# Graph-attention scores as 32-row products on four row groups, without head stacks

## What is computed

```python
q = (x @ Wq.T).reshape(b, n, NUM_HEADS, HEAD)        # 12 heads of 32
k = (x @ Wk.T).reshape(b, n, NUM_HEADS, HEAD)
bias = (spatial_encoding + edge_encoding)[:, None]   # adj + adj
scores = jnp.einsum('bqhd,bkhd->bhqk', q, k) * scale + bias
scores = jnp.where(row_nonzero, scores, -jnp.inf)
p = jax.nn.softmax(scores, axis=-1)
out = jnp.einsum('bhqk,bkhd->bqhd', p, v).reshape(b, n, h)
return out @ Wo.T + bo
```

## Time and profile before

| | us |
|---|---|
| median of 3 runs | 1613.49 (1613.08 to 1613.63) |
| the profiled execution, device time | 1610.95 |
| its span in the trace | 1608.7 |
| TensorE busy, of the span | 1530.1 (95%) |
| VectorE busy | 1247.8 (78%) |
| ScalarE busy | 900.9 (56%) |
| GpSimd busy | 470.3 (29%) |
| one group in the steady state, for example 801.05 to 848.64 | 47.59 |

### The profile page before, as it was taken

How to read it: one execution, slowest core, us unless ns; L and a number is a source line. 1 busy time by engine, 2 the same in 40 slices (tenths; PEclk the granted TensorE clock), 3 DMA queues, 4 the chain that set the end, 5 groups by cost and what they waited for, 6 DMA issues and landing times.

```text
span 1608.7 us, 38829 instructions
## 1 busy us (share of the span) xinstructions
PE 1530.1 (95%) x13760; PEld 1501.6 (93%) x13760; DVE 1247.8 (78%) x4559; ACT 900.9 (56%) x2091; POOL 470.3 (29%) x926
## 2 busy tenths in 40 slices
PE   4799999999999999999999999999999999999984
PEld 4799999999999999999999999999999999999973
DVE  6568887778887777888777888777788877788753
ACT  4556566556556555656655665655565665566531
POOL 4113332233323223333223332313333322332222
PEclk8799999999999999999999999999999999999986
DMA  8222022222112222212222211222221222221100
GB/s 246 61 63 71 31 51 73 70 73 73 49 39 63 74 70 73 67 30 55 74 70 73 73 44 44 64 71 72 73 65 30 57 73 70 74 73 35 40 10 10
DMA packets 84637, 101.66 MB, mean 63 GB/s; under 512 B 6640, under 2 KB 84208, under 8 KB 84448
## 3 DMA queue, kind: packets, MB, share of 16 engines
q1 hardware_dynamic: 83872, 98.20, 22.6%
q0 software_dynamic: 576, 0.99, 0.3%
HBM read 61.41 MB, written 37.75 MB: 62 GB/s over the span
## 4 chain that ended last, share of the span: by engine, by line
PE 90%; ACT 5%; DVE 2%; issue 1%; DMA 1%; POOL 1%; SPq 0%; DVEq 0%; ACTq 0%; POOLq 0%
PE bank L355 72%; PE bank L430 5%; PE bank L361 4%; PE bank L423 3%; PE bank L414 3%; ACT c_sb L556 3%; PE bank L436 1%; ACT qk L495 1%; PE bank L448 0%; DMA pT<-w 0%; DMA k<-qk_parts 0%; ACT prob L519 0%; DMA x_sb<-x 0%; DVE c_sb L645 0%; DVE weights L582 0%
## 5 line engine op out<-in xcount | busy, mean ns | idle before, releaser
L355 PE MATMUL bank<-h,weights 128*128 128x256 f32 x3456 | 429.8, 282 | 5.4 <-DVE h L758 5.0
L355 PEld LDWEIGHTS bank<-h,weights 128*128 128x128 f32 x3456 | 412.4, 190 | 6.4 <-issue 5.7
L519 ACT ACTIVATE prob<-prob,rmin 128x128 f32<-128x128 f32 x768 | 240.3, 390 | 13.3 <-DVE rmin L675 13.3
L355 PE MATMUL bank<-weights,h 128*128 128x384 f32 x1152 | 228.7, 343 | 0.0
L355 PE MATMUL bank<-hA,weights 128*128 128x256 f32 x1728 | 218.8, 281 | 1.5 <-DVE hA L606 1.5
L606 DVE TENSOR_TENSOR n<-bank,n 128x512 fp32r<-128x512 f32 x192 | 128.5, 683 | 109.9 <-ACT n L495 109.8
L355 PEld LDWEIGHTS bank<-hA,weights 128*128 128x128 f32 x1728 | 210.9, 189 | 1.9 <-DVE hA L606 1.9
L355 PEld LDWEIGHTS bank<-weights,h 128*128 128x128 f32 x1152 | 193.9, 188 | 0.0
L817 POOL TENSOR_SCALAR less_mean_gnn<-mv_gnn 128x2 f32<-128x2 f32 x64 | 14.4, 225 | 582.0 <-DVE mv_gnn L611 582.0
L495 ACT ACTIVATE n<-bank 128x512 fp32r<-128x512 f32 x192 | 113.9, 594 | 117.6 <-PE bank L355 117.6
L675 DVE CUSTOM_DVE_ANT_0 prob<-bank,adj_sb 128x128 f32<-128x128 f32 x768 | 174.5, 286 | 0.1
(11 more groups left out here) (109 smaller groups left out, 2660.3 us busy)
## 6 DMA issues: line engine op xcount, KB each, us to landing
qk_parts<-qk SPq DMA_DIRECT2D x96, 256.0 KB, 2.4
q<-qk_parts SPq DMA_DIRECT2D x96, 192.0 KB, 4.6
k<-qk_parts SPq DMA_DIRECT2D x96, 192.0 KB, 5.5
x_sb<-x SPq DMA_DIRECT2D x32, 384.0 KB, 4.1
out<-x SPq DMA_DIRECT2D x32, 384.0 KB, 2.5
adj_sb<-adj SPq DMA_DIRECT2D x32, 128.0 KB, 2.1
prob<-w SPq DMA_DIRECT2D x4, 576.0 KB, 7.2
x<-w SPq DMA_DIRECT2D x3, 576.0 KB, 4.8
```

The lines of the kernel that those rows point to most:

```text
L355: mm = pe.matmul(out, lhsT, rhs, start=(n == 0), stop=(n == len(pairs) - 1))
L519: e = act.activation(prob[:, j, h, :], prob[:, j, h, :], ACT.Exp, bias=rmin[:, j, h:h + 1], scale=-1.0)
```

## The change

The stacks in DRAM and the SBUF tiles `q3`, `k3` are gone, with all of their DMAs and waits. `qk` gets a second buffer, and `xn1`, which lay in it, a tile of its own. The scores of a graph are made by 36 products of 32 rows straight from the q and k parts of `qk`: head h = c*4 + a lies in rows 32a to 32a+31, so four products in a row go to four row groups and four banks; three of them in a bank (over n) sum up to a head. All 36 are issued at the fourth step of a graph (`S{j}3`); the first three only wait for their banks. A bank now holds the three heads of one row group, so scores, exps and transposed probabilities come in 4 jobs of 3 heads for each graph where there were 3 jobs of 4. Lists and banks are new on all engines.

```diff
-        qk = sb("qk", [P, 2, 2 * C, T], F16)
-        xn1 = qk[...]
-        qk_dram = nc.dram_tensor("qk_parts", [2, P, 2, 2 * C, T], F16).ap()
-        q3 = sb("q3", [3 * D, NH, T], F16)
-        k3 = sb("k3", [3 * D, NH, T], F16)
+        qk = sb("qk", [P, 2, 2, 2 * C, T], F16)
+        xn1 = sb("xn1", [P, G, H])
...
     "SP": [
-        ("k3", 1), ("ld_adj", 2), ("out", -1), ("qs0", 2), ("qs1", 2), ("qs2", 2), ("ld_x", 3), ("q3", 2)],
+        ("ld_adj", 2), ("out", -1), ("ld_x", 3)],
...
                 elif step[0] == "S":
-                    j, c = int(step[1]), int(step[2])
-                    pe.wait_ge(s_q3, STACKED * (g + 1))
-                    pe.wait_ge(s_k3, STACKED * (g + 1))
-                    for a in range(HC):
-                        mm = pe.matmul(bank(step)[:, a * P:(a + 1) * P], q3[:, a * C + c, j * P:(j + 1) * P], k3[:, a * C + c, j * P:(j + 1) * P], start=True, stop=True)
-                    mm.then_inc(full(step), 1)
+                    j, last = int(step[1]), int(step[2])
+                    if last == HC - 1:
+                        for k in range(3):
+                            wait_drained(pe, f"QK{k}", g)
+                        js = slice(j * P, (j + 1) * P)
+                        for c in range(C):
+                            for n, (u, v) in enumerate(PARTS):
+                                for a in range(HC):
+                                    rs = slice(a * D, (a + 1) * D)
+                                    mm = pe.matmul(bank(f"S{j}{a}")[:, c * P:(c + 1) * P], qk[rs, g % 2, u, c, js], qk[rs, g % 2, v, C + c, js],
+                                                   start=(n == 0), stop=(n == len(PARTS) - 1))
+                                    if (c, n) == (C - 1, len(PARTS) - 1):
+                                        mm.then_inc(full(f"S{j}{a}"), 1)
...
                 elif step[0] == "P":
-                    for a in range(HC):
-                        mm = pe.transpose(bank(step)[:, a * P:(a + 1) * P], prob[:, j, c * HC + a, :], ident[:, :])
+                    for c in range(C):
+                        mm = pe.transpose(bank(step)[:, c * P:(c + 1) * P], prob[:, j, c * HC + a, :], ident[:, :])
...
-                    lo(step, g, pT[:, LO, hs, :], pT[:, HI, hs, :], HC * P, "p (h q) -> p h q", h=HC)
+                    lo(step, g, pT[:, LO, a:NH:HC, :], pT[:, HI, a:NH:HC, :], C * P, "p (h q) -> p h q", h=C)
```

More of the change, by code:

```diff
@@ L71 @@
 BANK = {
-    0: ["S02", "C10", "N01", "P10", "C01", "V0"],
-    1: ["N10", "S00", "S12", "C11", "AT", "OT0"],
-    2: ["N12", "S01", "S10", "HL00", "QK1"],
-    3: ["HL11", "P00", "P11", "PV1", "QK2"],
-    4: ["HL10", "P01", "PV0", "HL01", "C00", "HTa"],
-    5: ["T2a", "N00", "U0", "T1b", "OT1", "WO1", "V1"],
-    6: ["N11", "U1", "N02", "P12", "WO0", "HTb"],
-    7: ["T2b", "S11", "P02", "T1a", "QK0"],
+    0: ["S01", "S13", "HL00", "WO0", "V0"],
+    1: ["C10", "N00", "P02", "P10", "QK1", "N10"],
+    2: ["N02", "S12", "P01", "P13", "HTb", "WO1", "T2a"],
+    3: ["V1", "N01", "P00", "PV0", "OT1", "N11", "U1"],
+    4: ["S00", "S10", "T1b", "P12", "QK2", "T2b"],
+    5: ["HL11", "C11", "S02", "HL01", "C00", "N12"],
+    6: ["HL10", "S03", "U0", "T1a", "P11", "HTa"],
+    7: ["AT", "S11", "P03", "C01", "OT0", "PV1", "QK0"],
 }
@@ L83 @@
     "SP": [
[1 row of a table removed]
+        ("ld_adj", 2), ("out", -1), ("ld_x", 3)],
     "PE": [
[5 rows of a table removed]
-    "ACT": [
[5 rows of a table removed]
-        ("HTb", 0)],
-    "DVE": [
[9 rows of a table removed]
[6 rows of a table added]
+    "ACT": [
[6 rows of a table added]
+    "DVE": [
[9 rows of a table added]
     "POOL": [
-        ("ln1", 2), ("ml", 0), ("gn1", -1), ("mu", 0), ("za0", -1), ("za1", -1), ("zb0", -1), ("xbo1", 2), ("xbo0", 2),
-        ("zb1", -1), ("gn0", 0), ("ln2", 1)],
+        ("xbo1", 2), ("ml", 0), ("gn1", -1), ("za1", -1), ("mu", 0), ("za0", -1), ("zb1", -1), ("zb0", -1), ("xbo0", 2),
+        ("gn0", 0), ("ln2", 1), ("ln1", 3)],
 }
-SPLIT_JOBS = (["T1a", "T1b", "QK0", "QK1", "QK2", "V0", "V1"] + [f"P{j}{c}" for j in range(G) for c in range(C)] +
+SPLIT_JOBS = (["T1a", "T1b", "QK0", "QK1", "QK2", "V0", "V1"] + [f"P{j}{a}" for j in range(G) for a in range(HC)] +
               ["OT0", "OT1", "T2a", "T2b"] + [f"N{l}{k}" for l in range(L) for k in range(3)] +
@@ L247, in build @@
         SPLIT_AFTER = {
-            "ACT": {"": (0,), "xn1_1": (1,), "T1b": (2, 3), "QK0": (4, 5), "QK1": (6,), "QK2": (7,), "V1": (8,), "V0": (9,)},
-            "DVE": {"ln1_ag": (0,), "T1b": (1, 2), "QK0": (3, 4), "QK1": (5,), "QK2": (6, 7), "V1": (8,), "V0": (9,)}}
+            "ACT": {"": (0,), "xn1_0": (1,), "T1b": (2, 3), "QK1": (4, 5), "QK2": (6,), "QK0": (7,), "V0": (8,), "V1": (9,)},
+            "DVE": {"ln1_ag": (0,), "T1b": (1, 2), "QK1": (3, 4), "QK2": (5,), "QK0": (6, 7), "V0": (8,), "V1": (9,)}}
         def staged(m):
@@ L300, in load_weights @@
                     sp.dma_start(staged(m), w_d[m].rearrange("(c p) o -> p c o", p=P)).then_inc(s_wload[STAGE_OF[m]], 16)
-            def stack(dst, s, which, parts, p):
-                for r, part in enumerate(parts):
-                    heads = qk_dram[p, :, part, which * C:which * C + C, :].rearrange("(a d) c t -> d a (c t)", d=D)
-                    sp.dma_start(dst[D * r:D * r + D, :, :].rearrange("d (a c) t -> d a (c t)", a=HC), heads).then_inc(s, 16)
             def run(step, g):
@@ L418, in run @@
                     wait_drained(pe, f"V{j}", g)
-                    for c in range(C):
-                        wait_drained(pe, f"P{j}{c}", g)
+                    for a in range(HC):
+                        wait_drained(pe, f"P{j}{a}", g)
                     for h in range(NH):
@@ L679, in run @@
                     j = int(step[2])
-                    for c in range(C):
-                        wait_drained(dve, f"S{j}{c}", g)
+                    for a in range(HC):
+                        wait_drained(dve, f"S{j}{a}", g)
                     dve.tensor_scalar(row0[:, j, :], rmin[:, j, :], 0.0, None, ALU.is_equal).then_inc(s_row0[j], 1)
@@ L763, in _ @@
                     split_weights(SPLIT_AFTER["DVE"].get(step, ()))
-                    if step == "QK1":
+                    if step == "QK2":
                         make_constants()
```

64 lines of the change are left out of this document (20 added, 44 removed), and 40 rows, old and new, of the table ORDER.

## The result

The changed kernel took 1638.28 us (median of 4 runs, 1636.87 to 1638.84) against 1613.28 for the kernel before (4 runs, 1610.75 to 1613.63): a ratio of 1.0157, with an interval of 1.0139 to 1.0175. That is +25 us where +55 had been forecast. The profiled execution took 1636.87 us (span 1635.1), 25.9 more than that of before, so the trace shows the difference in full.

What follows compares the result with a forecast made beforehand. TensorE was taken as the bound, busy 47.13 of 47.59 us a group. Terms of -52, +70, +56, -14 and -5 gave +55 us on the 1613.5 median, so 1668.5 us, with a range of 1622 to 1745.

Steps and rivals of the forecast that it cites:

- old scores go, new ones come: TensorE's scores: removing the old products saves 52 us, two blocks of 32-row products a group at 1.10 us add 70.
- stall behind U0: From U0's end to OT0, VectorE's list takes 8.65 us against TensorE's 6.89: 1.8 us a group lost, +56 us.
- wait at HTb goes: TensorE's wait at HTb for ScalarE's norm, 0.47 us in a usual group, disappears: -14 us.
- fill and drain of the pipeline: Two waits for the k stack while the pipeline fills, 9.0 us together, go and are partly replaced: -5 us.
- price of a 32-row product: Score blocks on TensorE: 25 ns a product, taken from PV's pairs, so 36 products take 0.90 us a block.
- Rival (a): Score blocks: four row groups truly at once, 53 ns a set, 0.60 us a block, 1636.5 us; chance 0.16.
- Edges: Entry to and exit from each score block on TensorE, where the kind of product changes: 0.20 us a block.
- x: The x load before ln1_st, asked for a few steps earlier: landing takes 4.1 us, 0.6 us of cover, costed at nothing.
- Rival (b): Score blocks: no overlap at all between row groups, 1.9 + 0.3 us a block, 1739.5 us; chance 0.14.
- rival (d): TensorE's granted clock falls to its lower level for part of each group, +100 us or more; chance 0.04.
- group of 49.3 us: Expected sign in the trace: a steady-state group takes 49.3 us, against 47.59 before.
- rival (c): Behind U0: VectorE's path is covered, no new stall, 1612.5 us, or 1580.5 with Rival (a) besides; chance 0.16.

Runs made afterwards that it cites:

- experiment 1: Changed kernel with a graph's 36 score products ordered by row group, all nine of one before the next: 1693.0 us.
- experiment 2: Changed kernel with score products alternating over two row groups at a time, 0 and 1 for 18 products, then 2 and 3: 1654.48 us.
- experiment 3: Changed kernel with only the HI by HI score products, 12 a graph instead of 36: 1619.68 us.
- experiment 4: Changed kernel with the first graph's 36 score products split into 12 before and 24 behind the two adjacency transposes: 1644.98 us.
- experiment 5: Changed kernel with VectorE's final additions y0 and y1 done on 32 of 384 columns: 1626.28 us.
- experiment 6: Changed kernel with T1b's HI half moved ahead of the exps x11 and x13 on ScalarE: 1638.22 us.
- experiment 12: Changed kernel with C01's drain late, T1b first on ScalarE, OT0's LO half ahead of the statistics, y0 and y1 on 32 of 384 columns: 1640.74 us.
- experiment 7: Changed kernel with C01's drain behind PV0.o on VectorE, OT0 in bank 0, T1b's LO half before PV0.r and T1b first on ScalarE: 1639.09 us.
- experiment 8: The kernel of experiment 7 with y1 and y0 also moved ahead of U0.m on VectorE: 1665.2 us.
- experiment 9: Changed kernel with V1 and its drains moved from behind U1 to behind P03, C10 behind N02, T2a's drain behind U1.dl: 1703.88 us.
- experiment 10: Changed kernel with V1 moved as in experiment 9, C01's drain late, T1b first, steps behind U1 reordered, OT0's drain before the statistics: 1675.74 us.
- experiment 11: The kernel of experiment 10 with P01 ahead of V1, and V0 and T2a out of VectorE's path behind U1: 1643.66 us.

## Why the forecast missed its size

The steps of the forecast, beside what the trace shows:

| part | forecast, us | measured, us |
|---|---|---|
| old scores go, new ones come | −52 + 70 = +18 | (1.50 − 1.63) x 32 = −4 |
| stall behind U0 | 1.8 x 31 = +56 | 1.6 x 31 = +50 |
| wait at HTb goes | −14 | −14 |
| fill and drain of the pipeline | −5 | −7 |
| sum | +55 | +25 (the span: +26.4) |

The fill's −7 is the difference of the spans, 26.4, less 30 groups of 1.12. The other rows come from one group; they give 1.0 of the 1.12 us, and where the last 0.1 a group goes wasn't traced. Of the 30 us between forecast and sum, 22 lie in the first row.

**The step that failed** is the price of a 32-row product, and with it the +70 us of the first row, which measured 1.50 x 32 = +48. The forecast took 25 ns, "the nearest row for how fast TensorE can start weight load and product pairs", from PV's 36 pairs in 0.91 us. That row is a rate of products one after another on all 128 rows, and says nothing on four groups side by side. It was taken as a floor on starts, and the floor isn't there between row groups: 14 ns a product, and 0.61 a block where 0.90 had been expected. Rival (a) had this mechanism, a set of four in the time of one (53 ns; 56 was measured). That its 1636.5 lies 2 us from the result is in part luck: its blocks at 0.60 with their edges came to 0.75 (+10 us), and a smaller stall (−6) and a shorter fill (−2) made up for it. Experiments 1 to 3 show it in three ways: a different order of the same products changes the time by the blocks' lengths and no more, and fewer products by theirs. The decisive sign was in the trace of before and was read too weakly: a 33-column PV product that can't come closer than 25 ns was seen to be limited by something that isn't its columns, and whether that something is one per array or one per row group was left to a guess, and the guess went the wrong way, 0.50 against 0.16.

**Edges.** 0.20 a block for the change of kind was about right: nine sets of 0.056 are 0.50, the blocks with what is late around them 0.75, so 0.25; experiment 4 gives 0.21 for a pair of changes.

**The stall** was right in its places and nearly in its size: 8.49 us against 8.65, 0.77 at C01 where 0.8 stood, 0.64 before OT0 where 1.0 stood. The two C took 1.34 where 1.06 was counted, and the steps ahead of C01 0.09 less than counted: together 1.60. U0.m started 0.29 after U0's end (0.30). HL00's drain was put at 0.45, where its row gives 0.41 and 0.47 was measured. VectorE had no idle time from there to PV0.o. That it is VectorE's list is shown by the trace, by experiment 5 (work taken away gives time back) and by 6 (ScalarE alone isn't it). ScalarE's list is right behind, as VectorE's waits in experiments 5 and 12 show; the forecast hadn't seen that.

**Fill and drain.** The −5 was forecast from the two waits, 9.0 us together, for the k stack and came out as −7, by luck and by another way. Those waits are gone, but others have come: outside of the 30 groups from the first AT to the last but one, TensorE is idle for 63.4 us where it was 65.0, only 1.6 less. It is busy there for 110.8 us where it was 116.0, though the work is about the same. What differs is the clock: the mean granted clock of the run is 0.987 (before: 0.978), and it stands at its lower level for 44 us of the span against 70, all in the first 78 and the last 81 us of either run. The forecast had no such term. Why the clock stays low for less time in the changed kernel, no run shows.

**HTb, x and the clock.** HTb starts at 830.43 without a wait; x lands in 3.3 and costs nothing; the granted clock is 1.00 in the group. Rival (b) falls with the 0.61 us of a block and with experiment 1, rival (d) with the clock of the group. The group of 49.3 us that the prediction names doesn't follow from its own terms, which give 47.59 + 0.56 + 1.8 − 0.47 = 49.5; 48.71 was measured. The lower end of its range, rival (a) with a stall of 1.5 and 4 us more gain in the fill, comes to 1623 and not 1622. Of rival (c), the other side, its own rule decided: at the price of (a) it needed a stall under 1.07 us, and the stall is 1.6. With the terms as measured, the bound is (4 + 14 + 7)/31 = 0.81 us a group.

**So the score products are a small gain**, by the rows of one group: 1.50 us in place of 1.63, three part products in place of one stacked, and no DMA round trip, which TensorE hardly waited for before. By this account the whole loss is in the new order, which puts U0 and its C products closer together than VectorE's list allows. The orders of experiments 7 to 12 moved the wait to C11, N00, P10, P12, WO0 or PV1, and none gained anything on the changed kernel. What stays open: the new score blocks in the old order, where 7.2 us of TensorE work lay between U0 and C, weren't tried, so that they would gain there is not shown. Nor is it shown which of VectorE's steps could leave this stretch without being missed elsewhere.

## What to carry to other kernels

Price products on separate row groups by the set, not by the product: a set of four costs what one costs, and each change to and from such products some 0.1 us on top. When two engines each run a fixed list, compare their sums of work between two hand-offs; where one is longer (8.2 us against 6.9 here), a moved step moved the wait here, and only less work took a part of it away (12 us). Cover, which is other work of the waiting engine put between the hand-offs, was needed where it came from in all three trials; whether cover that no other stretch needs would do, no run shows. And when a list is shortened, look at once for the engine behind it: of 0.7 us taken out of VectorE's list ScalarE's let only 0.34 through. A change that makes one part free can still lose by the order that it comes in, so its parts should be timed apart.
